# Attention stage of a two-layer recurrent kernel: row maximum taken in quarters, exp issued ahead of the previous tile's output steps

## The reference

```python
def _L1_attn_ref(x, W_qkv):
    qkv = jnp.einsum('bnd,ed->bne', x, W_qkv)
    q, k, v = ...                      # each [8, 2048, 1024]
    scale = DIM ** (-0.5)
    attn = jnp.einsum('bnd,bmd->bnm', q * scale, k)
    attn = jax.nn.softmax(attn, axis=-1)
    return jnp.einsum('bnm,bmd->bnd', attn, v)
```

## Time and profile before

| | |
|---|---|
| median of the two runs | 1608.11 us (1573.87 and 1642.36) |
| the profiled execution | 1574.44 us |
| its span on the slowest core | 1573.4 us |
| spans of the 8 cores | 1559.2 to 1573.4 us |
| mean granted clock of PE, slowest core | 0.936 |
| PE busy | 1287.7 us, 82% of the span |
| DVE, ACT, POOL busy | 493.3, 375.3, 141.5 us |
| chain that ended last | PE 69%, DVE 14%, ACT 8% |

### The profile page before, as it was taken

The page is one execution under the profiler, slowest core; times in us unless marked ns, Lnnn a source line. Parts: engine busy times, 40 slices in busy tenths (PEclk is TensorE's granted clock), DMA queues, the critical chain, the costliest instruction groups (busy, mean ns, idle before and its releaser), DMA issues.

```text
span 1573.4 us, 16620 instructions; the slowest of 8 cores (1559.2 to 1573.4 us)
## 1 busy us (share of the span) xinstructions
PE 1287.7 (82%) x6016; PEld 579.6 (37%) x6016; DVE 493.3 (31%) x479; ACT 375.3 (24%) x420; POOL 141.5 (9%) x236
## 2 busy tenths in 40 slices
PE   0587889999999999994345778888899878888886
PEld 0133334444444444442112333333344434444443
DVE  0614241001121144645487550133331122222222
ACT  1222211101111123232212445222102122223222
POOL 0011011001111100001000001000000101111111
PEclk9799999999999999997577999999999999999998
DMA  8333344255444646445433333532321223333322
GB/s 175 88 72 54 54 68 67 40 87 101 79 70 80 125 103 156 108 138 92 135 105 96 87 78 55 163 73 54 67 40 28 54 54 80 81 81 81 81 74 61
DMA packets 74160, 133.29 MB, mean 85 GB/s; under 512 B 23904, under 2 KB 32096, under 8 KB 72032
## 3 DMA queue, kind: packets, MB, share of 16 engines
q0 software_dynamic: 32384, 77.61, 28.3%
q1 hardware_dynamic: 33632, 42.03, 8.4%
q10 hardware_dynamic: 8064, 12.59, 2.2%
HBM read 159.47 MB, written 29.36 MB: 120 GB/s over the span
## 4 chain that ended last, share of the span: by engine, by line
PE 69%; DVE 14%; ACT 8%; DMA 4%; issue 3%; DVEq 0%; ACTq 0%; SPq 0%; POOL 0%; POOLq 0%
PE psf L347 10%; PE psf L353 9%; DVE BP L145 9%; PE psf L940 8%; PE psf L964 7%; PE psf L827 7%; PE psf L468 7%; ACT BP L145 6%; DVE FP L145 6%; PE psf L386 5%; PE psf L438 5%; PE psf L754 2%; PE psf L766 2%; PE psf L675 1%; PE psf L210 1%
## 5 line engine op out<-in xcount | busy, mean ns | idle before, releaser
L145 ACT ACTIVATE BP<-psf 128x512 bf16<-128x512 f32 (+1 forms) x208 | 144.6, 695 | 637.8 <-PE psf L353 305.3
L347 PE MATMUL psf<-BP 128*128 128x512 bf16 x768 | 187.1, 388 | 30.5 <-DVE BP L145 27.7
L353 PE MATMUL psf<-BP 128*128 128x512 bf16 x768 | 181.9, 380 | 0.0
L145 DVE TENSOR_TENSOR BP<-BP,psf 128x512 bf16<-128x512 bf16 x96 | 66.1, 688 | 368.2 <-ACT BP L145 367.5
L210 PE MATMUL psf<-BP,ones 128*128 128x512 bf16 x64 | 35.3, 551 | 117.1 <-ACT BP L145 107.2
L940 PE MATMUL psf<-BP 128*128 128x512 bf16 x512 | 128.3, 414 | 1.2 <-DVE BP L145 1.2
L347 PEld LDWEIGHTS psf<-BP 128*128 128x128 bf16 x768 | 75.8, 99 | 127.0 <-issue 41.4
L964 PE MATMUL psf<-BP 128*128 128x512 bf16 x512 | 115.0, 383 | 2.3 <-ACT BP L145 2.3
L827 PE MATMUL psf<-BP 128*128 128x512 bf16 x512 | 113.3, 382 | 3.8 <-DVE FP L145 3.8
L468 PE MATMUL psf<-BP 128*128 128x512 bf16 x512 | 111.8, 379 | 0.0
L353 PEld LDWEIGHTS psf<-BP 128*128 128x128 bf16 x768 | 75.3, 98 | 91.5 <-issue 1.8
(11 more groups left out here) (66 smaller groups left out, 1057.7 us busy)
## 6 DMA issues: line engine op xcount, KB each, us to landing
BP<-wg POOLq DMA_DIRECT2D x48, 256.0 KB, 3.9
BP<-wu POOLq DMA_DIRECT2D x48, 256.0 KB, 4.7
BP<-wd POOLq DMA_DIRECT2D x16, 768.0 KB, 8.9
FP<-xt SPq DMA_DIRECT2D x32, 256.0 KB, 8.5
FP<-xt SPq DMA_DIRECT2D x8, 1024.0 KB, 9.9
x1s<-FP SPq DMA_DIRECT2D x8, 1024.0 KB, 7.7
FP<-x1s SPq DMA_DIRECT2D x32, 256.0 KB, 6.4
FP<-x1s POOLq DMA_DIRECT2D x16, 512.0 KB, 6.4
```

What stands on the lines that cost most here:

```text
L145: ins = fn(*a, **k)
L347: te.matmul(pg, lhsT, rhs, start=(k == 0), stop=(k == NCH - 1))
L353: ins = te.matmul(pu, lhsT, rhs, start=(k == 0), stop=(k == NCH - 1))
```

## The change

Three things, all in the attention stage.

1. In `at_CD` the loops are exchanged: the group of 512 keys is now outside and the 8 partial sums inside, so that each bank is complete after 8 matmuls. PE adds to its semaphore after each group, not once at the end.
2. DVE takes a maximum over 512 columns after each group, into four columns of `FP` that were unused (`mxp`), and then the maximum of these four.
3. In the loop over the tiles `at_F(i)` is issued ahead of `at_GHJ(i - 1)`, not behind it.

```diff
@@ -933,19 +933,22 @@
             wt(te, s_s, exp_done[1])
             wt(te, s_v, tstate.get(("rm", 0), 0))
             wt(te, s_v, tstate.get(("rm", 1), 0))
-            for k in range(NCH):
-                lhsT = qt[:, k * 128:(k + 1) * 128]
-                for sps in range(4):
+            mxp = FP[:, F_MISC + par * 8 + 4: F_MISC + par * 8 + 8]
+            for sps in range(4):
+                for k in range(NCH):
+                    lhsT = qt[:, k * 128:(k + 1) * 128]
                     rhs = BP[:, R1 + k * T + sps * 512: R1 + k * T + sps * 512 + 512]
                     ins = te.matmul(psc[:, sps * 512: sps * 512 + 512], lhsT, rhs,
                                     start=(k == 0), stop=(k == NCH - 1))
-            inc(ins, s_t)
+                inc(ins, s_t)
+                wt(ve, s_t)
+                vx.reduce_max(mxp[:, sps:sps + 1],
+                              psc[:, sps * 512:(sps + 1) * 512], axis=AX.X)
             qt_free[par] = s_t.n
             mx = FP[:, F_MISC + par * 8: F_MISC + par * 8 + 1]
             bias = FP[:, F_MISC + par * 8 + 1: F_MISC + par * 8 + 2]
-            wt(ve, s_t)
             wt(ve, s_s, mx_free[par])
-            vx.reduce_max(mx, psc, axis=AX.X)
+            vx.reduce_max(mx, mxp, axis=AX.X)
             vx.tensor_scalar(bias, mx, -QSCALE, None, ALU.mult)
             tstate[("rm", par)] = s_v.n
 
@@ -1068,8 +1071,9 @@
             at_CD(i)
             if i >= 1:
                 at_E(i - 1)
+            at_F(i)
+            if i >= 1:
                 at_GHJ(i - 1)
-            at_F(i)
             at_I(i)
         at_AB(NTI - 1)
         at_E(NTI - 1)
```

## The result

| | before | changed |
|---|---|---|
| median, all runs | 1573.32 us (10 runs) | 1554.63 us (11 runs) |
| the profiled execution | 1574.44 us | 1553.39 us |
| its span, slowest core | 1573.4 us (core 0) | 1552.3 us (core 2) |
| attention on that core | 324.1 us | 304.9 us |
| attention, mean of the 8 cores | 323.8 us | 305.6 us |

The changed kernel takes 0.9887 of the time of before, 95% interval 0.9873 to 0.9902: 1.1% less. That is faster beyond the noise and within the 2% to which the prediction gave 0.87. The forecast was 1553.7 us. Both medians hold a few runs that were disturbed on one die (over 1600 us); the ratio is of the others.

A forecast was written before the change was run, and what follows sets the result against it. The prediction took PE's wait for ACT's late exp, plus lost clock, to bound the attention stage; 10.95 (waits) + 1.34 (quartered reduce) + 8.45 (clock) = 20.7 us off 1574.44 gave 1553.7 us, range 1545 to 1575.

The forecast's parts named there:

- What bounds the attention: Attention weight transposes (L911): PE waits 34.9 us in 16 waits for ACT, whose exp runs after E has ended.
- What is late next: At L916, after the exp's move: PE waits for DVE's multiply, so 0.73 us less per iteration, 10.95 us over 15.
- The start of the scores: CD, the score matmuls, follows L916 by 0.44 us, at +3.56 instead of +4.29 us after the output transposes start.
- The quartered reduce: DVE's row maximum in CD: 0.69 us per quarter, only the last behind CD; saves 1.34 us once, at tile 0.
- The order of the matmuls: In CD: the same 32 matmuls in the new order cost nothing, bounds 0 to 0.15 us.
- The clock: Score groups of tiles 2 to 15: 3 of 8 half-clock falls stay, 5 go at 1.69 us each, 8.45 us.
- The sum: Whole kernel: 10.95 + 1.34 + 8.45 = 20.7 us less than the profiled 1574.44 us, so 1553.7 us.
- A: Rival, attention: the clock falls as often as now and only waits are saved, 1562.1 us; chance 0.23.
- B: Rival, attention: the clock holds in all 14 score groups, 1548.6 us; chance 0.16.
- C: Rival, L916: DVE's multiply takes 1.96 instead of 1.23 us, the 0.73 is gone, 1573.1 us; chance 0.11.
- D: Rival, score groups: slower, clock down after the pause in every iteration and for longer, up to 1645 us; chance 0.05.

The follow-up runs named there:

- the kernel with 3.59: The changed kernel with the four waits of the first score matmul on ACT's and DVE's counters folded into two: 1553.16 us in one run.

## Why the prediction was right

- **What bounds the attention.** Right: the exp behind E's end was the wait. It is gone with the move alone.
- **What is late next.** Right, and the step on which most hung: L916 at +3.15 against the +3.12 worked out, a wait of 1.16 us for the multiply. The wait that went was 1.87 us and only 0.70 came through. Doubling the multiply moved L916 by the whole 1.33 us, so it is the multiply that ends the wait, without slack. The multiply kept its 1.23 us, but only 0.2 us of it ran beside L911's transposes, so the slowdown that bounded this term from below was hardly put to the test here; beside E's matmuls, with the output steps a tile later, it took 1.22.
- **The start of the scores.** Off by a little: +3.70, not +3.56. I had moved L916 and kept the 0.44 us behind it; PE's list of waits, hidden by 16 transposes before, outlasts 8 of them by 0.11 us. The term was 14 x 0.59 + 0.70 = 9.0 us instead of 10.95.
- **The quartered reduce.** Right: 0.69 us each, 0.16 for the maximum of four (2.9 us of DVE per tile where the whole reduce took 2.29, but all except the last quarter beside matmuls), PE's wait at tile 0 shorter by 1.34. In the steady state nothing shows that it is worth anything. What I missed is small: I had said that the group of tile 1 stays slow. It does stay over 7.0 us, but behind the shorter wait of tile 0 it took 7.6 us on the mean of the cores instead of 8.5.
- **The order of the matmuls.** Right: 6.9 us per group at full clock in either order.
- **The clock.** The direction was right, the number close: 4 slow groups kept where I had said 3. The term was 6.8 us instead of 8.45, partly because the pause is 3.70 and not 3.56 (the kernel with 3.59 kept 2 or 3). The supposition that I had made from the rows, that no fall comes once the new group is over 0.44 us old, gave a usable count and fits all traces: of the falls around the score groups of tiles 2 to 15, in any kernel and on any core, the latest came 0.46 us into a group. Why it should be so is not shown. The last E stayed slow, as said.
- **The sum.** 9.0 + 1.3 + 6.8 = 17.1 where the prediction had 20.7; the profiled execution fell by 21.05 (1574.44 to 1553.39), since tile 1's group gave 1.2 and some 2.8 (the group of tile 0 and 1.9, less 0.7) came from places where the two slowest cores merely differ. By the mean of the 8 cores the attention gained 18.2. So two terms that were a bit too large and luck in the rest make the forecast of 1553.7 look closer to 1553.39 than its working was.

On the rivals: A (the falls stay) was right in part, half of them stay. The passage of the Trainium skill that it leaned on ("TensorE: Matmul & The Clock Gate", the section on a second HAM failure mode) says that where PE idles briefly between groups of matmuls again and again, the clock swings between its levels. The traces agree in the attention, 8 or 9 of 14 groups before and 4 after, and add how much it depends on the pause: 0 of 14 at 0.89 us, 14 at 5.02. B (none stays) is what the fillers and the later output steps reach. C and D did not come about; D's direction, more slow groups with a longer pause, is what the doubled multiply shows.

## What to carry to other kernels

When a wait is taken away, work out what its engine waits for next before counting the wait as gain: here 0.70 of 1.87 us. Time between two groups of large matmuls can cost nearly as much again through the clock, as here, where 20 us of waiting became 36.5 us, so the order of small steps between two groups of matmuls is worth more than their busy times say: move them under the next group (43 us here), and if that can't be done, a few fillers that keep PE at work are cheap (6.3 us gained). Count the instructions between PE's last real wait and its next list of waits: if they are few, the list shows.

## What the runs showed of the hardware

- **Slow groups against the pause.** With usual pauses of 0.89, 3.59, 3.70, 4.29 and 5.02 us or more without a 512-column matmul, 0, about 3, 4, about 8 and 14 of 14 score groups were slow. The 24 transposes of 128 columns inside the pause did not prevent it; with four 512-column matmuls in its middle, which also took 0.86 us of idle time away, none was slow (0 of 14 at a total of 3.74 us). I had expected fewer falls, not a curve this steep between 3.6 and 5.0 us.
- **Waits on PE.** PE took up waits on semaphores that had long been reached 0.106 us apart. Two more of them cost 0.11 us behind 8 transposes (0.55 against 0.44 us), and nothing behind 16.
- **Reads beside writes.** DVE's multiply out of the lower bank of `psb` took 1.23 us with PE idle, 1.23 us with PE writing the upper bank during its first 0.2 us, and 1.22 us with PE writing `psf` beside the whole of it.
